# A four-layer graph network on one core: index rows spread by DMA in the slot steps, diagonals moved between engines, an index buffer of its own

## What is computed

```python
def _L2_gnn_ref(node_features, adjacency, W1, b1, g1, be1, W2, b2, g2, be2):
    m_j = jnp.einsum('bnd,do->bno', node_features, W1[:D])
    m_i = jnp.einsum('bnd,do->bno', node_features, W1[D:])
    pre = m_j[:, None, :, :] + m_i[:, :, None, :] + b1
    msg = jax.nn.gelu(_layernorm(pre, g1, be1), approximate=False)
    agg = jnp.einsum('bijo,bij->bio', msg, adjacency)
    upd_in = jnp.concatenate([node_features, agg], axis=-1)
    return _layernorm(upd_in @ W2 + b2, g2, be2)
```

## Time and profile before

| | us |
|---|---|
| median of 3 runs | 4087.21 (4080.77 to 4090.16) |
| the profiled execution | 4083.3 |
| its span | 4081.4 |
| busy: PE, DVE, ACT, POOL | 3302.0, 3378.2, 2785.5, 2108.6 |

### The profile page before, as it was taken

One profiled execution on the slowest core, in us unless ns is written; L12 is line 12 of the kernel. 1 busy time (PEld: TensorE's weight loads), 2 busy tenths in 40 slices (PEclk: granted clock), 3 DMA queues, 4 the chain that ended last, 5 costly groups with the idle time before them and its releaser, 6 DMA issues.

```text
span 4081.4 us, 93269 instructions
## 1 busy us (share of the span) xinstructions
PE 3302.0 (81%) x25274; PEld 2780.7 (68%) x25556; DVE 3378.2 (83%) x12271; ACT 2785.5 (68%) x6381; POOL 2108.6 (52%) x1923
## 2 busy tenths in 40 slices
PE   3484688887888888888798888888887887988898
PEld 2273567677676777767677776767776676776777
DVE  4788888898888888888888888888898888887830
ACT  2484676858667586776858676685868768595753
POOL 1182663718547292753729274471827547192730
PEclk7596899989899999999999999999999999999999
DMA  2000001000010100001010000101000010000000
GB/s 81 26 1 26 1 1 42 1 22 21 1 43 1 43 0 22 22 1 43 1 35 9 22 22 1 43 1 43 0 22 22 1 43 1 27 0 1 16 1 21
DMA packets 95513, 73.89 MB, mean 18 GB/s; under 512 B 7504, under 2 KB 95184, under 8 KB 95184
## 3 DMA queue, kind: packets, MB, share of 16 engines
q1 hardware_dynamic: 95184, 70.09, 5.7%
HBM read 61.68 MB, written 8.39 MB: 17 GB/s over the span
## 4 chain that ended last, share of the span: by engine, by line
issue 26%; POOL 25%; DVE 21%; PE 16%; ACT 6%; DVEq 3%; POOLq 2%; ACTq 0%; DMA 0%; SPq 0%
POOL v_z L511 18%; POOL v_diag L517 3%; PE n_bank_d L1599 3%; PE n_bank_d L1600 3%; PE n_bank_c L1582 3%; DVE v_normed L971 2%; PE n_bank_d L1596 2%; POOL v_prstd L525 2%; DVE v_top_at L1043 2%; PE n_bank_b L1660 1%; DVE v_top L1040 1%; PE n_bank_d L1496 1%; ACT v_pair L842 1%; DVE v_adj_x L1048 1%; POOLq L532 1%
## 5 line engine op out<-in xcount | busy, mean ns | idle before, releaser
L511 POOL TENSOR_TENSOR v_z<-v_z,all_bc_L_gnn_be 128x512 f32<-128x512 f32 x620 | 786.2, 1269 | 22.0 <-DVE v_z L1093 22.0
L525 POOL TENSOR_TENSOR v_prstd<-v_pvar,all_neg_half 128x8 f32<-128x8 f32 x310 | 563.5, 1818 | 267.8 <-DVE v_pvar L1109 240.0
L1496 PE MATMUL n_bank_d<-v_diag,v_msg 128*128 128x128 f32 x4960 | 637.1, 284 | 32.2 <-ACT v_diag L740 32.2
L1496 PEld LDWEIGHTS n_bank_d<-v_diag,v_msg 128*128 128x128 f32 x4960 | 594.8, 197 | 35.2 <-ACT v_diag L740 35.2
L740 ACT ACTIVATE v_diag<-all_ident,v_value 128x128 f32<-128x128 f32 x1860 | 572.5, 386 | 0.0
L1485 PE MATMUL n_bank_b<-v_parts,v_onehot 128*128 128x128 f16 x5472 | 374.0, 224 | 152.6 <-ACT n_bank_b L682 152.6
L1485 PEld LDWEIGHTS n_bank_b<-v_parts,v_onehot 128*128 128x128 f16 x5472 | 332.7, 100 | 224.7 <-ACT n_bank_b L682 183.5
L1582 PE MATMUL n_bank_c<-all_l_wsd,v_fT 128*128 128x256 f32 x1792 | 449.1, 392 | 31.4 <-ACT v_adjT L667 28.9
L1485 PE MATMUL n_bank_c<-v_parts,v_onehot 128*128 128x128 f16 x4960 | 346.9, 226 | 141.7 <-ACT n_bank_c L682 141.6
L1485 PEld LDWEIGHTS n_bank_c<-v_parts,v_onehot 128*128 128x128 f16 x4960 | 308.6, 101 | 213.2 <-ACT n_bank_c L682 168.4
L677 ACT ACTIVATE v_fT<-n_bank_d,all_l_c 128x256 f32<-128x256 f32 x256 | 119.7, 474 | 447.1 <-PE n_bank_d L1600 446.9
(11 more groups left out here) (281 smaller groups left out, 7344.6 us busy)
## 6 DMA issues: line engine op xcount, KB each, us to landing
v_adj_l<-in_adj SPq DMA_DIRECT2D x128, 256.0 KB, 3.7
v_adj_x<-in_adj SPq DMA_DIRECT2D x64, 256.0 KB, 3.4
v_ring<-in_x SPq DMA_DIRECT2D x16, 512.0 KB, 5.9
out_x<-v_xout SPq DMA_DIRECT2D x64, 128.0 KB, 2.0
w_wu<-in_L_gnn_wu SPq DMA_DIRECT2D x4, 192.0 KB, 2.5
all_W<-in_L_gnn_W SPq DMA_DIRECT2D x2, 128.0 KB, 4.3
w_raw<-in_L_gnn_ws SPq DMA_DIRECT2D x1, 192.0 KB, 3.0
w_raw<-in_L_gnn_wd SPq DMA_DIRECT2D x1, 192.0 KB, 3.1
```

What stands on the lines that cost most here:

```text
L511: nc.gpsimd.tensor_tensor(z[par][:, units], z[par][:, units], wide(bc["L2_gnn_be1"])[:, units], ALU.add).then_inc(sem["z_ready"], 1)
L525: nc.gpsimd.tensor_tensor(prstd[:], pvar[:], minus_half, ALU.pow).then_inc(sem["prstd_ready"], 1)
L1496: ins = nc.tensor.matmul(ps_agg[:, u // NB, (u % NB) * P:(u % NB + 1) * P], msg[par][:, u], diag[par][:, u], start=False, stop=False, skip ...
```

## The change

Four parts:

- **Index rows by DMA.** PE's product and ACT's copy are gone from steps and mixed stage. `keep_index` writes one chunk of 128 slots to `indexT`, SP stores it to DRAM (`slot_rows`, a row of 1024 indices for each slot), and then reads one row for all 128 partitions for each slot (`spread_out`), into two buffers. `pick` waits for that DMA. SP has a slot stage of its own.
- **Diagonals.** ACT makes all eight; POOL none.
- **Variance scaled sooner.** `pvar` is made ahead of the second half's normalisation, and `prstd` has two buffers. ACT waits for the two halves one by one, with the gelu between them.
- **Index memory.** `index` has memory of its own and is cleared once, at the start. POOL's memset and the wait for it leave the mixed stage.

```diff
-BY_ACT = 6
...
-        indexT = plan.sb("indexT", [P, CHUNKS, UNITS * P], BF16)
-        at = plan.take(UNITS * 3 * P * 2)
-        parts = plan.view("parts", [P, UNITS, 2, D], at, F16)
-        index = plan.view("index", [P, UNITS, CHUNKS * P], at, BF16)
+        indexT = plan.sb("indexT", [P, UNITS * P], BF16)
+        parts = plan.sb("parts", [P, UNITS, 2, D], F16)
+        index = plan.sb("index", [P, UNITS * SLOTS + CHUNKS * P - SLOTS], BF16)
...
-        spread = plan.sb("spread", [P, UNITS * P], BF16)
+        spread = plan.sb("spread", [P, 2, UNITS * P], BF16)
...
-        prstd = plan.sb("prstd", [P, UNITS])
+        prstd = plan.sb("prstd", [P, 2, UNITS])
...
+        slot_rows = nc.dram_tensor("slot_rows", (CHUNKS * P, UNITS * P), BF16, kind="Internal").ap()
...
+            def spread_out(slot, par):
+                sp.dma_start(spread[:, par], slot_rows[bass.ds(slot, 1)].broadcast_to((P, UNITS * P)))\
+                    .then_inc(spread_in[par], 16)
+
+            def first_spreads(a, again):
+                sp.wait_ge(sem["slots_ready"], a + 1)
...
+                with sp.Fori(0, chunks) as c:
+                    sp.wait_ge(sem["index_kept"], first + c + 2)
+                    sp.sem_inc(keep["held"], 1)
+                    sp.dma_start(slot_rows[bass.ds(c * P, P)], indexT[:]).then_inc(index_stored, 16)
+                sp.reg_add(stored, stored, chunks)
+                sp.wait_ge(index_stored, sp.snap(stored) * 16 + 16)
+                sp.sem_inc(keep["held"], 1)
+                if again:
+                    sp.wait_ge(sem["onehot_ready"], sp.snap(count) + a * 2)
+                    sp.sem_inc(keep["held"], 1)
+                for par in range(2):
+                    spread_out(par, par)
+
+            def slots(a):
+                pairs = sp.snap(n_pairs)
+                before = sp.snap(sp.snap(count) + a * 2)
+                with sp.Fori(1, pairs + 1) as i:
+                    for par in range(2):
+                        sp.wait_ge(sem["onehot_ready"], before + (i * 2 + par))
+                        sp.sem_inc(keep["held"], 1)
+                        spread_out(i * 2 + par, par)
+                sp.reg_add(count, count, pairs * 2)
...
                     load_extract(g + 2)
+                if l1:
+                    first_spreads(g + 1, again)
...
             with sp.Fori(1, GROUPS - 3) as g:
                 mix(g)
+                slots(g + 1)
...
-                def diagonals(par, steps, slot):
-                    pool.wait_ge(sem["summed"], steps * 2 + 2)
-                    for u in range(BY_ACT, UNITS):
-                        ins = nc.gpsimd.tensor_tensor(diag[par][:, u], ident[:],
-                                                      value[:, u, bass.ds(slot, 1)].broadcast_to((P, P)), ALU.mult)
-                    ins.then_inc(sem["diag2_ready"], 1)
...
-                if l1:
-                    if u:
-                        pool.wait_ge(sem["agg_done"], g + 1)
-                        pool.sem_inc(keep["held"], 1)
-                    nc.gpsimd.memset(index[:], 0.0).then_inc(sem["index_cleared"], 1)
...
-            def keep_spread(g, ahead):
-                act.wait_ge(sem["spread_made"], ahead + (g + 1))
-                nc.scalar.activation(spread[:], ps_spread, ACT.Copy).then_inc(sem["spread_kept"], 1)
...
-                    nc.scalar.activation(indexT[:, bass.ds(c, 1)].rearrange("p a n -> p (a n)"), ps_index,
-                                         ACT.Copy).then_inc(sem["index_kept"], 1)
+                    act.wait_ge(index_stored, (first + c) * 16 + 16)
+                    nc.scalar.activation(indexT[:], ps_index, ACT.Copy).then_inc(sem["index_kept"], 1)
...
-                    for u in range(BY_ACT):
+                    for u in range(UNITS):
                         ins = nc.scalar.activation(diag[par][:, u], ident[:], ACT.Copy,
                                                    scale=value[:, u, bass.ds(slot, 1)])
...
-                def act_step(par, step, slot, first=False, second=False):
-                    ahead = act.snap(step + g * 2 + 2)
-                    act.wait_ge(sem["onehot_ready"], ahead)
-                    keep_spread(g, ahead)
-                    if not (first or second):
+                def act_step(par, step, slot, second=False):
+                    act.wait_ge(sem["z_made"], step * 2 + 1)
+                    seed(1 - par, 0)
+                    if not second:
                         gelu(par, act.snap(step - 1), 1)
...
+                    act.wait_ge(sem["z_made"], step * 2 + 2)
+                    seed(1 - par, 1)
+                    gelu(1 - par, step, 0)
+                    diagonals(1 - par, step, slot - 1)
...
             def pick(ahead, par):
-                dve.wait_ge(sem["spread_kept"], ahead + 1)
+                dve.wait_ge(spread_in[par], (ahead + (2 - par)) * 8)
...
-                        if not first:
+                        if half_ == 0 and not first:
                             dve.wait_ge(sem["prstd_ready"], step + 1)
-                            dve.wait_ge(sem["msg_ready"], step * 2 + (half_ + 1))
-                            normalise(1 - par, half_)
+                            dve.wait_ge(sem["msg_ready"], step * 2 + 1)
+                            normalise(1 - par, 0)
                     dve.wait_ge(sem["stats_done"], step * 2 + 2)
                     v.tensor_scalar(pvar[:].rearrange("p (q u) -> p q u", u=2), pstats[:, par, :, :, 2], 1.0 / D, UP * UP * LN_EPS,
                                     ALU.mult, ALU.add).then_inc(sem["pvar_ready"], 1)
+                    if not first:
+                        dve.wait_ge(sem["msg_ready"], step * 2 + 2)
+                        normalise(1 - par, 1)
                     pick(dve.snap(step + g * 2 + 2), par)
```

105 lines of the change are left out of this document (42 added, 63 removed).

## The result

| | before | changed |
|---|---|---|
| median, us | 4086.04 (4080.77 to 4090.16, 6 runs) | 4104.18 (4102.31 to 4107.31, 6 runs) |
| span of the profiled execution | 4081.4 | 4100.6 |

The ratio is 1.0045, 95% interval 1.0032 to 1.0058: slower by 0.45%, 18 us, where 31 us less were forecast. I go through the places in the order of the prediction. A *power* is POOL's operation that makes `v_prstd`, one in each step; lengths of steps and stages are taken from power to power.

The account below looks back on a forecast made before the run. The prediction took POOL's work and a ring over POOL and DVE to bound the slot step. From 4083.3 us: - 51 + 66 - 5 - 37 - 5 = 4051, or 4055 against the median; forecast range 4015 to 4095, wide range 3985 to 4340.

Parts of the forecast that it names:

- The step: Settled step of the slot stage: 4.93 us against 5.115, DVE without idle time, 51 us less in all.
- this ring: Slot step: POOL's power, DVE's normalisations and statistics, scaling, next power; said to fill the 5.12 us step exactly.
- The head: Start of a slot stage: the third pick's index row queues behind stores and loads, 66 us more in all.
- less 5 at the start: Start of a slot stage: the old copy and product leave ACT and PE, 5 us less over 16 groups.
- The transfer: Index row by DMA in each slot step: lands 2.7 us after issue, hidden between picks.
- rival 1: Slot steps: one row read 128 times is slow, step 6.6 us, 4550 us in all; chance 0.25.
- Rival 2: Slot steps: the pick is held by POOL's power, step 5.7 us, 4270 us in all; chance 0.05.
- The addition stays, the memset does not: 14 x 2.65 = 37 us less: Mixed stage: DVE's line 971 no longer waits through POOL's memset in fourteen groups; bounds nothing to 60 us.
- Rival 3: Slot steps: ACT comes late, the step stays at 5.1 us and heads cost the rest, about 4100 us; chance 0.07.

Follow-up runs that it names:

- the two runs that undo one part each: Changed kernel with two of eight diagonals made by POOL again: 4113.3 us; changed kernel with the variance scaled behind the second half's normalisation again: 4086.8 us.
- Rows ahead: Changed kernel with the loop's first index row asked for ahead of the mixed stage's stores and loads, later rows one pick sooner: 4053.9 us, ratio 0.9907.
- the products by zeros: Changed kernel with dummy TensorE products of zeros in two gaps of each mixed stage, ten at +71 us and five at +132 us: 4069.7 us, ratio 0.9950.
- all of it: Changed kernel with index rows asked for earlier, products by zeros in five places, and x loaded behind the next row: 3949.6 us, ratio 0.9649.

## Why the prediction was wrong

- **The step: right.** 4.894 us against 4.93, DVE without idle time, the scaling still held. 64 us in place of 51, since the first steps of a group gain too and the step is 0.04 shorter. The reason given was half right: that a step needs both parts to be shorter ("only if both POOL's work and this ring are") is refuted by the two runs that undo one part each. POOL's four operations were added up as if end to end; they overlap by 0.05 to 0.18 us, and so were not the exact bound they seemed.
- **The head: right.** 66 us were forecast, less 5 at the start; 68 were measured. Rows ahead gave 50 us back, with the first step down to 4.4 us, so its place in the queue is the cause.
- **The transfer: right.** It lands 3.1 us after issue (median), where 2.7 was taken and 3.76 was the limit. One row of 2 KB read 128 times is not slow, and rival 1 falls.
- **Rival 2 falls.** Two picks last 0.87 us beside a power. By the rule of the Trainium skill ("SBUF — State Buffer", "Who interferes with whom") the pick would wait for it. The trace disagrees for the power, and agrees for the addition, which held the scaling to 0.67 us and a late pick to 1.41.
- **The failed step: "The addition stays, the memset does not: 14 x 2.65 = 37 us less".** DVE did gain the time (its normalisation ended 2.4 us sooner), but it ended at the next wait for PE. Only in the two mixed stages without layer 3 or without layer 0 did something of it stay: they fell from 139.71 to 135.56 and from 137.98 to 135.37 us, of which the memset put back took 1.3 and 1.8 us again. The prediction named that case as its bound ("nothing, if PE's pair products are late instead") and had the row on which it rests, PE at 0.50 through the pair products, but took the other value because the chain that ended last runs through line 971. A chain shows one path; the second, within a microsecond of it, is not in it (last pair term of group 5 at +54.5 us behind PE's slow products, at +53.7 behind the memset without them).
- **The term that was missing: TensorE's clock elsewhere in the stage.** Moved work was priced by its length and its cover alone. Nothing was priced for the clock of PE falling at moments where it had not fallen before, at +73 and +134 us. This cost 2.4 us in each of the nine like stages beyond the lost saving, and the products by zeros took 3.1 us back. The mixed stages came out 17 us longer in place of 42 shorter. This difference of 59 us is more than the whole miss of 49 in the medians; the other terms came out some 7 us better than forecast.
- The direction was forecast wrong: faster had a chance of 0.59. The forecast of 4015 to 4095 us does not hold 4104, and none of the rivals named this cause. The wide range of 3985 to 4340 us holds it by luck, since it was stretched upward for rivals 1 to 3, and none of them happened. Rival 3 gave "about 4100 us" from a step that gains nothing, which the step of 4.89 us excludes: the number is right by chance.

Open: why the clock falls behind one idle time of 2.61 us and not behind the same one elsewhere; what the index rows by DMA alone do to the step; and which of the three parts of "all of it" brought its 8 us.

## What to carry to other kernels

Before you price a wait that is taken away, ask what ends the next wait behind it, and count nothing for it while an engine that runs slow there is as late. Where TensorE waits and is then slow, look at its granted clock behind each gap and try products by zeros in the gap, into a free bank: here they were worth 34 and 55 us, together more than the 64 us of the shorter step. In the kernel before, where the memset held DVE too, they brought 0.3% and let the clock fall elsewhere: measure them, and look at the clock of the whole stage again. A prefetch into two buffers must be asked for as soon as its buffer is free, ahead of the bulk loads in its queue.
